# Graph attention kernel: the small TensorE products of the batch loops made 128 rows or 88 columns wide

## The reference

```python
def gat_layer(x, src, dst, W, a_src, a_dst, bias, heads, out_ch):      # layers 0 and 1
    xW = (x @ W).reshape(n, heads, out_ch)
    e = leaky_relu(sum(xW * a_src)[src] + sum(xW * a_dst)[dst], 0.2)
    w = exp(e - segment_max(e, dst)[dst])
    return segment_sum(xW[src] * (w / segment_sum(w, dst)[dst]), dst) + bias
# layer 2: h = x @ W.T; the score of an edge has one term more
enc = relu(edge_attr @ edge_W.T + edge_b)                              # 53125 x 256
alpha = leaky_relu(sum(h[src]*a_src) + sum(h[dst]*a_dst) + sum(enc * h[dst]), 0.2)
# then the same softmax over the edges of a destination and the same weighted sum
```

## Time and profile before

| | us |
|---|---|
| runs | 2092.95, 2092.96, 2096.61 |
| profiled execution: its own time | 2100.78 |
| its span, from the first instruction to the last | 2099.0 |
| loop of layer 0, about | 110 to 645 |
| loop of layer 1, about | 725 to 1290 |
| layer 2 with its start, about | 1345 to 2050 |

### The profile page before, as it was taken

One profiled execution on the slowest core, in us unless ns is written; L12 is line 12 of the kernel. 1 busy time (PEld: TensorE's weight loads), 2 busy tenths in 40 slices (PEclk: granted clock), 3 DMA queues, 4 the chain that ended last, 5 costly groups with the idle time before them and its releaser, 6 DMA issues. The chain is left out here.

```text
span 2099.0 us, 43225 instructions
## 1 busy us (share of the span) xinstructions
PE 1673.1 (80%) x9241; PEld 1064.7 (51%) x9241; DVE 1574.9 (75%) x4409; ACT 1370.3 (65%) x5004; POOL 1504.7 (72%) x1648
## 2 busy tenths in 40 slices
PE   7377778777876577878878877789999999999984
PEld 5244445545544344545545444445565655565652
DVE  5567877777778456666656667879899998899997
ACT  3267776777675444545545446668888888888886
POOL 3677777777767577777777773667777777777873
PEclk9578877888787767777777787779999999999995
DMA  7655554555641344444444641434444444444431
GB/s 195 173 161 143 145 143 139 142 144 167 186 116 37 118 129 135 134 129 135 137 129 134 197 121 39 122 109 125 125 129 130 127 130 127 125 128 133 137 90 61
DMA packets 130636, 274.39 MB, mean 131 GB/s; under 512 B 39701, under 2 KB 65274, under 8 KB 130367
## 3 DMA queue, kind: packets, MB, share of 16 engines
q0 software_dynamic: 64128, 181.33, 32.1%
q1 hardware_dynamic: 61564, 86.45, 13.5%
q10 hardware_dynamic: 4699, 3.86, 0.7%
HBM read 255.00 MB, written 17.20 MB: 130 GB/s over the span
## 5 line engine op out<-in xcount | busy, mean ns | idle before, releaser
L1283 POOL DMA_INDIRECT rows<-table,index_all x1100 | 1073.7, 976 | 402.9 <-issue 304.9
L1801 PE MATMUL bank<-rows,onehot 128*128 128x264 f32 (+1 forms) x2200 | 863.2, 492 | 55.0 <-DVE rows L843 17.4
L854 DVE TENSOR_TENSOR sums<-sums,bank 128x264 f32 (+1 forms) x1320 | 556.8, 422 | 325.6 <-PE bank L1801 252.5
L1498 ACT ACTIVATE rows<-rows,wgt 128x33 f32<-128x33 f32 (+2 forms) x2740 | 706.3, 338 | 2.1 <-issue 1.1
L1801 PEld LDWEIGHTS bank<-rows,onehot 128*128 128x128 f32 x2200 | 416.7, 230 | 126.1 <-issue 77.7
L1721 PE MATMUL bank<-identb,onehotT 128*128 128x128 bf16 x1320 | 228.9, 261 | 41.9 <-issue 28.9
L1283 POOL DMA_INDIRECT late<-table,index_all x220 | 214.1, 973 | 67.0 <-issue 62.2
L1721 PEld LDWEIGHTS bank<-identb,onehotT 128*128 128x128 bf16 x1320 | 135.1, 117 | 155.0 <-issue 93.6
L1506 ACT ACTIVATE prod<-bank 128x512 f32<-128x512 f32 x240 | 134.1, 559 | 107.2 <-PE bank L1813 97.0
L1820 PE MATMUL bank<-late,onehotT 128*128 x1320 | 201.0, 290 | 1.3 <-DVE prod L863 1.3
L1450 ACT CAST onehot<-bank 128x768 f32<-128x768 bf16 x240 | 174.5, 729 | 40.5 <-PE bank L1721 40.3
(11 more groups left out here) (215 smaller groups left out, 2242.2 us busy)
## 6 DMA issues: line engine op xcount, KB each, us to landing
locb<-loc_d SPq DMA_DIRECT2D x120, 352.0 KB, 3.8
rows<-table,index_all POOLq DMA_INDIRECT x1100
flags<-flags_d SPq DMA_DIRECT2D x508, 27.5 KB
late<-table,index_all POOLq DMA_INDIRECT x220
table<-rows SPq DMA_DIRECT2D x25, 136.0 KB, 1.8
table<-rows SPq DMA_DIRECT2D x25, 134.0 KB, 2.7
late<-table SPq DMA_DIRECT2D x1, 3300.0 KB
table<-rows SPq DMA_DIRECT2D x25, 129.5 KB, 2.3
```

Of the source, the lines that this page charges most:

```text
L854: done(v.tensor_tensor(a, a, sum_bank(l, t, s)[:, 0:VV], ALU.add), "add")
L1283: g.indirect_dma_start(out=rows_of(l, t)[:, s, 0:ROW[l]], out_offset=None, in_=table[l], in_offset=bass.IndirectOffsetOnAxis(ap=index_all[ ...
L1498: i = a.activation(r, r, ACT.Copy, scale=wgt[:, t.u, h * B + s:h * B + s + 1])
L1801: done(m.matmul(sum_bank(l, t, s)[:, 0:VV], onehot[:, t.u, s, :], rows_of(l, t)[:, s, 0:VV], start=True, stop=True), "agg")
```

## The change: what it does

- `runs`, `linkrow`, `scale`, `carry` and `edgew3` get 128 partitions in place of 1, 1, 2, 2 and 30, and `attrT` is taken over 128 partitions. Rows that are not used are zero on one side of the product (`scale`, `edgew3`, or the zeros of the identity).
- `endsT`: the stationary operands are the identity (128*128), and 128 neighbouring columns of `top` over 88 rows, whose first column is the wanted one. `top` is re-ordered for that (last, next, first). As PE now reads the `next` part too, DVE's wait for `endp` moves from `tops2` ahead of the first scan in `tops`.
- `cols`: 128*88 against one column of the identity. `factor`: 128 rows. `scoresT` and `weightsT` take 88 columns and 88 rows in every layer. `encode`'s first product has 128 rows.
- At the start: four memsets more on DVE, one more on POOL with a wait for it.

```diff
-        carry = sb("carry", [2, RING, P])
+        carry = sb("carry", [P, RING, P])
-        runs = sb("runs", [1, 2, 8 * (B + 1)])
-        linkrow = sb("linkrow", [1, 2, 8 * B])
+        runs = sb("runs", [P, 2, 8 * (B + 1)])
+        linkrow = sb("linkrow", [P, 2, 8 * B])
-        scale = sb("scale", [2, 8])
+        scale = sb("scale", [P, 8])
-        edgew3 = sb("edgew3", [30, D], BF16)
+        edgew3 = sb("edgew3", [P, D], BF16)
-        attrT = lateb[0:30, BLOCKS * 3 * D:].rearrange("p (r f) -> p r f", r=RING)
+        attrT = lateb[:, BLOCKS * 3 * D:].rearrange("p (r f) -> p r f", r=RING)
+        LINES = 8 * B
+        ps_leftw = ps_T[:, 256:256 + 8 * (B + 1)].rearrange("p (h s) -> p h s", h=8)
+        ps_rightw = ps_T[:, 352:352 + LINES]
+        LAST, NEXT, FIRST_T = 0, 1, 2
+        topw = top[:, :, :].rearrange("p i e -> p (i e)")
...
+            for unused in (score[:, :, :], expT[:, :, :], top[:, :, :]):
+                ch(v.memset(unused, 0.0))
+            ch(v.memset(edgew3[:, :], 0.0))
...
+                    need(dve, "endp", kk)
+                    done(v.tensor_tensor_scan(top[0:R, NEXT, :], flags[0:R, t.u, PEN_F, :], s0, -BIG,
                                               ALU.add, ALU.max), "topf")
 
                 def tops2(t, l=l, H=H):
...
-                    need(dve, "endp", kk)
...
+            g.memset(scale[:, :], 0.0).then_inc(p_zero, 1)
...
-            g.memset(scale[:, :], 1.0).then_inc(p_pool, 1)
+            pool.wait_ge(p_zero, 1)
+            g.memset(scale[0:2, :], 1.0).then_inc(p_pool, 1)
...
-                        r = m.transpose(ps_T[0:H * B, i * P:(i + 1) * P], score[:, i, 0:H * B], ident[:, :])
+                        r = m.transpose(ps_T[0:LINES, i * P:(i + 1) * P], score[:, i, :], ident[:, :])
...
-                    m.matmul(left[:, :, 0], ones[0:1, :], runs[0:1, 0, 0:H * (B + 1)].rearrange(
+                    m.matmul(ps_leftw[:, 0:H, 0], ident[:, :], runs[:, 0, 0:H * (B + 1)].rearrange(
                         "p (h s) -> p h s", h=H)[:, :, B], start=True, stop=True)
-                    m.transpose(left[:, :, 1:], top[0:H * B, 2, P - 1:P],
-                                ident[0:H * B, 0:H * B])
-                    r = m.transpose(ps_right[:, 0:H * B], top[0:H * B, 2, 0:1], ident[0:H * B, 0:H * B])
+                    m.transpose(ps_leftw[:, :, 1:], topw[:, P - 1:2 * P - 1], ident[0:LINES, 0:LINES])
+                    r = m.transpose(ps_rightw, topw[:, 0:P], ident[0:LINES, 0:LINES])
...
-                        r = m.matmul(ps_col[0:H * B, i:i + 1], linkrow[0:1, i, 0:H * B], ones[0:1, :], start=True, stop=True)
+                        r = m.matmul(ps_col[:, i:i + 1], linkrow[:, i, :], ident[:, 0:1], start=True, stop=True)
...
-                    m_ = m.transpose(ps_e[:, WT:WT + H * B], expT[0:H * B, 0, :], ident[0:H * B, 0:H * B])
+                    m_ = m.transpose(ps_e[:, WT:WT + LINES], expT[:, 0, :], ident[0:LINES, 0:LINES])
```

More of the change, by code:

```diff
@@ L317, in gat_kernel @@
         s_bias = sem("s_bias")
-        p_pool, p_dve, p_pe = sem("p_pool"), sem("p_dve"), sem("p_pe")
+        p_pool, p_dve, p_pe, p_zero = sem("p_pool"), sem("p_dve"), sem("p_pe"), sem("p_zero")
         s_dpad = sem("s_dpad")
@@ L769, in tops @@
                     if SELF[l]:
-                        done(v.tensor_tensor(top[0:R, 0, :], s0, scoreT[0:R, 1, :], ALU.max), "top0")
+                        done(v.tensor_tensor(top[0:R, FIRST_T, :], s0, scoreT[0:R, 1, :], ALU.max), "top0")
                         need(dve, "top0", kk + 1)
-                        s0 = top[0:R, 0, :]
-                    done(v.tensor_tensor_scan(top[0:R, 1, :], flags[0:R, t.u, PEN_F, :], s0, -BIG,
+                        s0 = top[0:R, FIRST_T, :]
+                    need(dve, "endp", kk)
+                    done(v.tensor_tensor_scan(top[0:R, NEXT, :], flags[0:R, t.u, PEN_F, :], s0, -BIG,
                                               ALU.add, ALU.max), "topf")
@@ L779, in tops2 @@
                     need(dve, "topf", kk + 1)
-                    need(dve, "endp", kk)
-                    done(v.tensor_tensor_scan(top[0:R, 2, ::-1], flags[0:R, t.u, PEN_B, ::-1], top[0:R, 1, ::-1],
+                    done(v.tensor_tensor_scan(top[0:R, LAST, ::-1], flags[0:R, t.u, PEN_B, ::-1], top[0:R, NEXT, ::-1],
                                               -BIG, ALU.add, ALU.max), "top")
@@ L807, in finish_tops @@
                     done(v.scalar_tensor_tensor(seg[0:R, :], flags[0:R, t.u, PEN_L, :], ps_col[0:R, 0:1],
-                                                top[0:R, 2, :], ALU.add, ALU.max), "seg1")
+                                                top[0:R, LAST, :], ALU.add, ALU.max), "seg1")
                     need(dve, "seg1", kk + 1)
@@ L1128, in meta @@
                     chains(t)
-                    sp.dma_start(carry[:, t.u, :], carry_d[bass.ds(t.k * B, 1), :, :].rearrange("a r e -> (a r) e")).then_inc(s_meta[l][t.u], 16)
+                    sp.dma_start(carry[0:2, t.u, :], carry_d[bass.ds(t.k * B, 1), :, :].rearrange("a r e -> (a r) e")).then_inc(s_meta[l][t.u], 16)
                 def self_rows(l=l):
@@ L1759, in endsT @@
                     need(pe, "top", kk + 1)
-                    left = ps_left[:, 0:H * (B + 1)].rearrange("p (h s) -> p h s", h=H)
-                    m.matmul(left[:, :, 0], ones[0:1, :], runs[0:1, 0, 0:H * (B + 1)].rearrange(
+                    m.matmul(ps_leftw[:, 0:H, 0], ident[:, :], runs[:, 0, 0:H * (B + 1)].rearrange(
                         "p (h s) -> p h s", h=H)[:, :, B], start=True, stop=True)
-                    m.transpose(left[:, :, 1:], top[0:H * B, 2, P - 1:P],
-                                ident[0:H * B, 0:H * B])
-                    r = m.transpose(ps_right[:, 0:H * B], top[0:H * B, 2, 0:1], ident[0:H * B, 0:H * B])
+                    m.transpose(ps_leftw[:, :, 1:], topw[:, P - 1:2 * P - 1], ident[0:LINES, 0:LINES])
+                    r = m.transpose(ps_rightw, topw[:, 0:P], ident[0:LINES, 0:LINES])
                     done(r, "endp")
@@ L1788, in weightsT @@
                         need(pe, "sc1", kk + 2)
-                    m_ = m.transpose(ps_e[:, WT:WT + H * B], expT[0:H * B, 0, :], ident[0:H * B, 0:H * B])
+                    m_ = m.transpose(ps_e[:, WT:WT + LINES], expT[:, 0, :], ident[0:LINES, 0:LINES])
                     if SELF[l]:
                         need_apart(pe, ("mask", kk + 1))
-                        m_ = m.transpose(ps_e[:, QT:QT + H * B], expT[0:H * B, 1, :], ident[0:H * B, 0:H * B])
+                        m_ = m.transpose(ps_e[:, QT:QT + LINES], expT[:, 1, :], ident[0:LINES, 0:LINES])
                     done(m_, "wp")
```

## The result

The changed kernel takes 2074.28 us (median of four runs, 2069.99 to 2076.86) against 2092.95 (2090.33 to 2096.61) for the kernel before beside it: ratio 0.9904, 95% interval 0.9883 to 0.9926. Forecast were 2070 us and 2058 to 2086. The profiled execution took 2075.92 us (span 2074.1), against 2100.78 (span 2099.0): 24.9 us less.

The account below looks back on a forecast made before the run. Layer 2 was taken as bound by PE's sums releasing a nearly full POOL. Terms -24.3 and -3 make -27 us: 2073.5 from the profiled execution or 2066 from the median; 2070 was taken, range 2058 to 2086.

Parts of the forecast that it names:

- Layer 2's bound: Layer 2: POOL, nearly as full as PE, waits for PE's sums; without 24.3 us of waiting, 16.41 us per batch.
- PE needs 1.2 us less per batch: Layer 2, PE: net saving per batch, mostly six `encode` groups at 0.20 us each; bounds +0.2 to -1.4.
- 0.17 us as an aside: Layer 2, PE: `cols` and `factor` save 0.17 us per batch, 0.10 at `cols`' entry and 0.07 in `factor`.
- whether the clock still falls once a batch hardly matters: Layer 2: a half-clock stretch costs PE 1.3 us, about what the change leaves spare.
- Rival 2: Layer 2: the clock falls more often as PE idles; 2084 us at 1.2 stretches per batch, 2119 at two; chance 0.08.
- Start of layer 2: Between 1345 and 1437: some 24 `encode` groups save PE 4.8 us; taken as -3 us, range 0 to -5.
- Layers 0 and 1: Half-clock `endsT`, `cols`, `factor` add about 0.4 us per batch net, covered by PE's idle time: cost 0, range -1 to +6.
- Rival 4: Layer 0 ends later, PE falling behind a few tenths per batch from the start: +10 us, 2080; chance 0.02.
- the cover: Layer 0: PE's 67.8 us of idle time covers the added work; without it 32 us at most.
- Wait and memsets: DVE's earlier wait for `endp` costs 0; the start's memsets cost 0, or up to 2 us without cover.
- The rule set against the change: Skill's rule: loads overlap matmuls only in different row groups; by it layer 2 would gain nothing or lose. The prediction disagreed.

Follow-up runs that it names:

- rest_only: The whole change, but with `encode`'s first product left on 30 rows: 2073.12 us, ratio 0.9906 to the kernel before.
- enc65: The kernel before with `encode`'s first product alone widened, to 65 rows: 2080.75 us, ratio 0.9924.
- ends_only: The kernel before with the changed `endsT` alone (wide operands, `top` re-ordered, DVE's wait moved): 2100.31 us, ratio 1.0022.
- own_a: The change widened in rows only, old columns kept, with one of POOL's four layer 2 slots moved to DVE: 2062.08 us, ratio 0.9837 to the kernel before.
- enc_only: The kernel before with `encode`'s first product alone on 128 rows: 2072.0 us, ratio 0.9905.
- cols_only: The kernel before with `cols` and `factor` alone contracting over 128 rows, their columns as before: 2068.94 us, ratio 0.9868.

## Why the prediction was right, and where its reasons were wrong

**Layer 2's bound.** Right that layer 2 was held up by PE's sums, that the waits go and that POOL's own work is next: 16.27 us per batch against the 16.41 forecast, -29.2 us against -24.3. POOL's groups divide the -29.2: its idle time ahead of the gathers fell from 133.1 to 109.0 us, by 24.1, which are the waits that the prediction had at 24.3; the gathers themselves fell by 5.1, and these it had as unchanged. With PE out of the way the period falls to what POOL needs whichever way PE gets faster; that is why the time came out. That the total is so close (24.9 us less in the profiled executions, 27 forecast) is luck in part: layer 2's batches gave 4.9 us more than forecast, layers 0 and 1 cost 7.1 us, and the two nearly cancel.

**Which part of the change.** Wrong. The step that failed is "PE needs 1.2 us less per batch", nearly all of it `encode`'s six groups. The delays are as large as read (0.10 + 0.09 us, gone with 65 rows), but rest_only keeps them and loses nothing. Of the 29.2 us, by the two kinds of batches on PE: 16 batches touched by a half-clock stretch x 1.41 = 22.6, and 34 batches x the 0.18 by which clean ones got shorter = 6.1. POOL's side says much the same: in the 18 of its batches that a stretch touches it waited 24.1 us beyond the bare issue, in the 16 others 0.1. So the first part is the clock. The second comes with `cols` and `factor` alone, two steps to which the prediction gave 0.17 us as an aside, and it isn't waiting for PE: POOL waits for nothing beyond the bare issue in clean batches, before or after, and its gathers got shorter.

**The clock.** Wrong: "whether the clock still falls once a batch hardly matters". It was the larger part. The mistake was to set the cost of a stretch against PE's spare time of a whole batch. The stretches begin behind `factor`, and there nothing is spare: enc65 pays 1.0 us for each with 1.1 us freed. Rival 2 had the clock as a danger, behind narrow products, which is the right place, and with the wrong sign.

**Start of layer 2.** -2.9 us against -3; POOL waits there 11.8 us, five times, against 15.4, six times.

**Layers 0 and 1.** Mis-sized: +7.1 us against 0 (-1 to +6). Rival 4, given 0.02, came true beside the forecast: the last sum of layer 0 ends at 679.3 in place of 672.9. (The six kernels that leave layer 0's steps as they were took 569.7 to 574.3 us for it in their profiled executions, so 579.2 lies outside that spread, but the size of the loss isn't sharp.) Half-clock `endsT` of layer 0, answering to the earlier trace rows:

```profile
208.45 0.56 PE L1771 MATMUL bank<-runs,ident 128*128 128x4 f32 x2 [0.59 <-DVE top L790]
208.87 0.39 PE L1773 MATMUL bank<-ident,top 88*128 88x88 f32 x1
209.05 0.35 PE L1774 MATMUL bank<-ident,top 88*128 88x88 f32 x1
209.20 0.42 PE L1732 MATMUL bank<-identb,onehotT 128*128 128x128 bf16 x2
```

0.75 us in place of 0.36: +0.39, where the prediction had +0.52. `cols` takes 0.51 us (211.60 to 212.11) in place of 0.38, and `factor` 0.43 (to 212.54) in place of 0.52: +0.13 and -0.09, for +0.26 and -0.08. So the added work was no more than forecast; the cover did not hold. PE's wait for the scores, from 100 to 640, after the earlier trace rows:

```profile
PE bank L1763 <- DVE score L766: 74.6, 36, 2.7
```

There was idle time enough, and there still is, but it stands ahead of `scoresT`, and a sum over the loop doesn't say that `endsT` can use it. From batch 3 to batch 17 layer 0 took 202.5 us in place of 191.7, with 86 us at half clock in place of 68; how much of that is `endsT` and how much is where the clock's stretches fell stays open, since ends_only and rest_only show other sums (572.0 and 575.4).

**Wait and memsets.** The first gather of layer 0 stands at 57.2 in place of 58.4: nothing, as forecast.

**The rule set against the change** (full-size products lose an overlap) failed here as the prediction thought: `encode`'s last product and the first of `hnode3` follow each other at 0.11 us with their loads hidden. A sentence of the Trainium skill that the prediction did not use bears on the delays: TensorEngine Tiling (Array Packing), Key Properties, says that a change of tiling mode drains TensorE. The traces agree in kind: with 64 rows or fewer, and with 44 columns, a full-size neighbour stands some 0.09 us further off ahead and 0.07 to 0.09 behind; with 65 rows and 88 columns it doesn't. That these products enter such a mode no run shows.

**Clean batches** stand at 16.4 us in the kernels with one-row `cols` (without the added products) and at 16.24 in the others (16.18 in own_a), and POOL's gathers account for it: in clean batches the eleven take 10.78 us in the kernel before and 10.77 in enc_only, but 10.63 in the change and 10.62 in cols_only, while its multiplications and gaps stay the same. It is the tenth gather of a batch that is longer in the first two (below). Why the narrow `cols` puts that gather beside DVE's multiplication isn't shown.

What isn't settled is why the clock stays up. Narrow products just ahead of the stretch are one reading: cols_only, which changes that place alone, leaves one stretch of fifteen. But enc_only leaves `cols` and `factor` as they were and has none, while enc65, with no delay at `encode` either, has eight.

## What to carry to other kernels

Read a clock that falls once per batch by its place before its price: find the products just behind which it falls, and ask whether PE has time to spare at that point, not in the batch as a whole. Widen such products in rows, where zeros cost nothing here (`cols` takes 0.26 us with 128 rows, 0.34 with one), and leave their columns of weights as they are; a load of 128 columns for one wanted column is paid at half clock (`endsT` 0.75 us in place of 0.36). And before a sum of small savings on a busy engine is believed, see by a kernel that forgoes them whether they are on the chain at all. Work moved off a full engine can come back to it as longer instructions: in own_a less than half of the 0.64 us moved was won, and most of that went into the gathers.

## What the runs showed of the hardware

- 64 rows, or 44 columns, delay a product by 0.094 us behind a full-size one (0.316 to 0.318 us from the second half of a sum, against 0.222) and delay its successor by 0.07 to 0.09; 65 rows and 88 columns don't.
- The delay and the clock are two things. Rows of `encode` and half-clock stretches in 34 batches, each from one profiled execution: 30 rows 15, 64 rows 11, 65 rows 8, 128 rows none.
- POOL's gather takes 1.22 us in place of 0.95 when it starts beside DVE's multiply of two SBUF operands; in the kernel before this is the tenth gather of nearly every batch, here one of them:

```profile
1965.53 0.42 DVE L843 TENSOR_TENSOR rows<-rows,wgt 128x264 f32<-128x264 f32 x1
...
1965.56 1.22 POOL L1283 DMA_INDIRECT rows<-table,index_all  x1 [0.30 <-issue]
```

That holds for 33 of 34 batches. In cols_only the tenth gather mostly stands elsewhere, and takes 0.95 in 24 of 34. In own_a a multiplication on POOL that starts beside the same kind of DVE instruction takes 0.93 us in place of 0.63. The Trainium skill, GPSIMD Engine Reference, Specifications, says that POOL shares its SBUF interfaces with VectorE and contends with instructions that have two SBUF inputs; the trace agrees, at 0.27 us for one gather.
